# Products of zeros ahead of transposes and in waits of TensorE, in the third stretch of a two-layer decoder kernel

## The chip, the cores and the metric

The kernel runs on one core of a Trainium2 chip. The metric is the device time of one execution in microseconds (us), the median of some runs. TensorE does the matrix products and transposes, VectorE (DVE), ScalarE (ACT) and GpSimd (POOL) do the rest, SyncE (SP) issues most of the transfers. The profile also shows the clock that was granted to TensorE, as a share of 2.4 GHz; in each record it is either 1.0 or 0.5, that is 2.4 or 1.2 GHz.

## The reference

The input is 16 sequences of 128 tokens with 256 channels. Two layers follow each other, and each adds three blocks to the running x:

```python
x = x + L0_attn(layernorm(x))              # a gated convolution block
x = x + L0_xattn(ctx, layernorm(x), ctx)   # attention, queries from ctx
x = x + L0_ffn(layernorm(x))               # 32 experts, the best 2 of each token
x = x + L1_attn(layernorm(x))              # 16 causal heads
x = x + L1_xattn(layernorm(x), ctx, ctx)   # one wide head with an added bias
x = x + L1_ffn(layernorm(x))               # attention with rotary, then 8 experts
```

The change lies in the second layer. Its first block is causal attention in which the softmax is taken twice: once to find the entropy of each row, then again with the scores multiplied by a temperature that is a polynomial of that entropy.

```python
sim = einsum('bhid,bhjd->bhij', q, k) / sqrt(hd); sim = where(causal, neg, sim)
p = softmax(sim); entropy = -sum(p * log(p + 1e-9))
beta = where(entropy > 0.5, maximum(poly(entropy), 1.0), 1.0)
out = einsum('bhij,bhjd->bhid', softmax(sim * beta), v) @ Wo.T + bo
```

Its third block begins with a causal attention without temperature, with rotary position factors, and ends with 8 experts of which each token takes 2.

## The kernel before

The program has three stretches. The first does the first two blocks of layer 0, the second the 32 experts. The third (`phase_c`, line 1578) does all of layer 1 and starts about 671 us after the first instruction; near its end the tiles of the 8 experts follow (`Tiles`, line 2314), which end the program.

The third stretch works on eight pairs g = 0 to 7, two sequences each. A pair passes through six parts, and each part has a program of its own for each engine: `first` (norm, transposes, the products q, k and v), the attention `one` with temperature, `mix` (output product, the wide-head attention), `rotary` (norm, q, k and v of the third block), the attention `two`, and `last` (output product, gate of the experts). The transposes of `first`, `mix`, `rotary` and `last` are those of line 253; the products with the weights have lines 272 and 281.

An attention works through four units u = 0 to 3 of a pair (`UNITS`, line 286): one sequence and half of the heads each, so eight heads. For one unit TensorE does, in `causal_tensor` (line 1444):

- `sc`: the mask by two bf16 products (line 1466) and the scores by two f32 products (line 1468) into two banks of its result memory;
- `tr`: eight transposes of the exponentials (line 1486) into the same two banks;
- `pv`: eight products with the values (line 1498), into the bank `bs`;
- `ot`: two transposes back (line 1504).

Between them VectorE takes the maximum (line 1523), divides an earlier output (lines 1537 and 1539) and subtracts the maximum (line 1529); ScalarE takes the exponential (line 1556), copies the transposed exponentials out of the banks (line 1559) and copies the output (line 1563). In attention `one` there is more between the subtraction and the last exponential: ScalarE's exponential and logarithm (lines 1762 and 1767), VectorE's sums (lines 1779 and 1784), and on GpSimd two wide products (lines 1796 and 1799), ten small operations of the polynomial (lines 1802 to 1817) and the wide product with the temperature (line 1820).

All units of attention `one` share one pair of banks. So the scores of unit u of the next pair can be written only when the transposes of unit u of this pair have been copied out, and the transposes of unit u + 1 only when VectorE has subtracted the maximum from those scores (lines 1478 to 1484). In the first two pairs this gives a fixed turn: transposes of unit u of pair 0, copy, values, scores of unit u of pair 1, maximum, subtraction, transposes of unit u + 1 of pair 0.

Each engine's order is fixed: `emit` and `weave` (lines 104 to 115) merge the programs of all parts by the times of the table `AT_C` (line 1297), and the engines then run in that order; the table's times are used for nothing else. An f32 product stands in the trace as two records, a transpose as one.

`keep_warm(c, con, n, bank)` (line 1082) issues n products of a tile of zeros with itself, 128x128 by 128x256 in f32, into a bank whose content is not read after it. The kernel before has 37 of them: at the start of the program, around the border of the second and third stretch, and in the first pairs.

Of the kernel before, what the change touches and what calls it, by code (L numbers as in the profile page):

```python
# [24 lines left out]
NG = NSEQ // GS  # L25
# [34 lines left out]
class Tally:  # L60
# [9 lines left out]
    def at(self, n, j=None):  # L70
        return self.sem, self.base + self.step * (self.per * n + (self.per if j is None else j + 1))
# [32 lines left out]
def weave(plans):  # L104

    plans = [[next(p, None), p] for p in plans]
    while plans := [x for x in plans if x[0] is not None]:
        first = min(plans, key=lambda x: x[0])
        yield first[0]
        first[0] = next(first[1], None)  # L110
# [971 lines left out]
def keep_warm(c, con, n, bank=7):  # L1082

    for _ in range(n):
        c.nc.tensor.matmul(c.ps[:, bank, 0:D], con["zero"][:, 0:P], con["zero"][:, 0:D], start=True, stop=True, skip_group_check=True)
# [355 lines left out]
    return tally.at(n, j)  # L1441


def causal_tensor(c, l, con, g, at, woven):


    pe, ps = c.nc.tensor, c.ps

    def scores(u):
        s, ch = UNITS[u]  # L1450
        b0 = l.place(g, u).b0
        yield at("sc", u)
        if u == 0:
            pe.wait_ge(*l.q_in.at(g))
            pe.wait_ge(*l.k_in.at(g))
        if woven:
            if u:
                pe.wait_ge(*l.dd.at(g, u - 1))
            if g:
                pe.wait_ge(*l.pt_in.at(g - 1, u))  # L1460
        elif u == 1 and l.apart(g):
            pe.wait_ge(*l.other.pt_in.at(g))
        elif u or g:
            pe.wait_ge(*earlier(l.pt_in, g, u, 2 if u and l.apart(g) else 1))
        for b in range(2):
            pe.matmul(ps[:, b0 + b, :], con["ident_bf"], con["mask"], start=True, stop=True, skip_group_check=True)
        for b in range(2):
            m = pe.matmul(ps[:, b0 + b, :], l.qt[64 * b:64 * b + 64, ch, P * s:P * s + P], l.kp[64 * b:64 * b + 64, ch, :, P * s:P * s + P],  # L1468
                          start=False, stop=True, tile_position=(64 * b, 0), skip_group_check=True)
        m.then_inc(*l.sc.up())  # L1470
        if woven and g == 0 and u == 1:
            keep_warm(c, con, 2, 5)

    def values(u):
        s, ch = UNITS[u]
        d, there = l.d[u % l.n_d], l.place(g, u)
        yield at("tr", u)
        pe.wait_ge(*l.ee.at(g, u))
        if woven and u == 0:
            pe.wait_ge(*l.dd.at(g))  # L1480
        elif woven:
            pe.wait_ge(*l.pt_in.at(g, u - 1))
            if g + 1 < NG:
                pe.wait_ge(*l.dd.at(g + 1, u - 1))
        for h in range(NU):
            m = pe.transpose(ps[:, there.b0 + h // 4, P * (h % 4):P * (h % 4) + P], d[:, h, :], con["ident"])  # L1486
        m.then_inc(*l.tr.up())
        yield at("pv", u)
        pe.wait_ge(*l.pt_in.at(g, u))
        if u == 0:  # L1490
            pe.wait_ge(*l.v_in.at(g))
        if u == 1 and l.apart(g):
            pe.wait_ge(*l.other.ao_in.at(g))
        elif g or u:
            pe.wait_ge(*earlier(l.ao_in, g, u, 2 if u and l.apart(g) else 1))
        for h in range(NU):
            r, half = h % 4, h // 4
            m = pe.matmul(ps[32 * r:32 * r + 32, there.bs, P * half:P * half + P], l.vv[:, s, NU * ch + h, :], d[:, h, :],  # L1498
                          start=True, stop=True, tile_position=(0, 32 * r), skip_group_check=True)
        m.then_inc(*l.pv.up())  # L1500
        yield at("ot", u)
        pe.wait_ge(*l.os_in.at(g, u))
        for half in range(2):
            m = pe.transpose(ps[:, there.bs, P * half:P * half + P], there.os[:, P * half:P * half + P], con["ident"])
        m.then_inc(*l.ot.up())

    def in_order(part):
        for u in range(len(UNITS)):
            yield from part(u)

    yield from weave([in_order(scores)] + [values(u) for u in range(len(UNITS))])


# [64 lines left out]
def phase_c(c, con, dram, persist, w, arena, results, tables, tiles, xd_zero):  # L1578
# [7 lines left out]
    tick = lambda g: (lambda piece, u="": AT_C["%s%s" % (piece, u)][g])  # L1586
    tick_b = lambda g: (lambda piece, u: AT_C["%s%db" % (piece, u)][g])
    TOP, MIX = 7, 6
    with ExitStack() as ctx:
# [85 lines left out]
        def first_tensor(g):  # L1675
            at = tick(g)
            yield at("t0")
            if g == 0:
                pe.wait_ge(*comb.at(g))
                keep_warm(c, con, 3)  # L1680
                pe.wait_ge(*first.mean.at(g))
                keep_warm(c, con, 2)
            pe.wait_ge(*first.xn.at(g))
            if g:
                pe.wait_ge(*one.v_in.at(g - 1))
            if g >= 4:
                pe.wait_ge(*lg_in.at(g - 4))
                if g % 2:
                    pe.wait_ge(*router.pr_in.at(g // 2 - 2))
            turn_rows(c, first, con, x_first)  # L1690
            yield at("q")
            pe.wait_ge(*first.xt_in.at(g))
            by_channel(c, TOP, w.wa[:, 0, :, :], first.xt).then_inc(*qpj.up())
            yield at("k")
            pe.wait_ge(*one.q_in.at(g))
            by_channel(c, TOP, w.wa[:, 1, :, :], first.xt).then_inc(*kpj.up())
            yield at("v")
            pe.wait_ge(*one.k_in.at(g))
            by_token(c, TOP, w.wa[:, 2, :, :], first.xt).then_inc(*vpj.up())

# [254 lines left out]
        def rotary_tensor(g):  # L1955
            at = tick(g)
            yield at("t3")
            pe.wait_ge(*rot.xn.at(g))
            turn_rows(c, rot, con, x_rms)
            yield at("rk")  # L1960
            pe.wait_ge(*rot.xt_in.at(g))
            for k in range(KD):
                m = pe.matmul(ps[:, MIX, 0:GT], w.wk[:, k, :], rot.xt[:, k, :], start=(k == 0), stop=(k == KD - 1), skip_group_check=True)
            m.then_inc(*rk.up())
            yield at("rr")
            pe.wait_ge(*kr_in.at(g))
            for ch in range(KD):
                m = pe.matmul(ps[:, MIX, GT * ch:GT * ch + GT], w.rep[0:4 * HD, ch, :], kr[0:4 * HD, :], start=True, stop=True, skip_group_check=True)  # L1968
            m.then_inc(*rr.up())
            for half in range(2):  # L1970
                yield at("rq%d" % half)
                if half == 0:
                    pe.wait_ge(*two.k_in.at(g))
                else:
                    pe.wait_ge(*rq_half.at(g))
                by_channel(c, MIX, w.wf[:, half, :, :], rot.xt).then_inc(*rq.up())
            yield at("rv")
            pe.wait_ge(*two.q_in.at(g))
            by_token(c, MIX, w.wv, rot.xt).then_inc(*rv.up())
# [66 lines left out]
        def last_tensor(g):  # L2046
            at = tick(g)
            yield at("t5")
            pe.wait_ge(*two.ao_in.at(g))
            pe.wait_ge(*one.v_in.at(min(g + 3, NG - 1)))  # L2050
            if g:
                pe.wait_ge(*lg_in.at(g - 1))
                if g == NG - 2:
                    pe.wait_ge(*tables.cnt_in.at(0))
                if g % 2 == 0 or g == NG - 1:
                    pe.wait_ge(*router.pr_in.at((g + 1) // 2 - 1))
            turn_rows(c, last, con, two.ao)
            yield at("o2")
            pe.wait_ge(*last.xt_in.at(2 * g))
            by_token(c, TOP, w.wf[:, 2, :, :], last.xt).then_inc(*oj2.up())  # L2060
            yield at("t6")
            pe.wait_ge(*rows_in.at(g))
            turn_rows(c, last, con, rows[g % 2][:, :, 0:D])
            yield at("gate")
            pe.wait_ge(*last.xt_in.at(2 * g + 1))
            by_token(c, TOP, w.gw, last.xt).then_inc(*lg_mm.up())
# [92 lines left out]
                        in_=rows[s // GS][:, s % GS, :], in_offset=None).then_inc(*s_disp[s // GS].up())  # L2159

        def tensor_program(g):
            yield from weave([first_tensor(g), causal_tensor(c, one, con, g, tick(g), True), mix_tensor(g), rotary_tensor(g),
                              causal_tensor(c, two, con, g, tick_b(g), False), last_tensor(g)])

        def vector_program(g):
            yield from weave([first_vector(g), causal_vector(c, one, g, tick(g), mix.turned.at(2 * g - 2) if g else None, temperature_vector(g)),
# [36 lines left out]
        def tables_tensor():  # L2203
            for n, choice in enumerate((NROUND - 2, len(CHOICES) - 1)):
                yield settled[n] + LATE * n
                pe.wait_ge(*router.pr_in.at(choice))
                pe.wait_ge(*meta.at(choice))
                tables.count_tensor(c, con, total, TOP)
# [511 lines left out]
```

## Time and profile before

| | us |
|---|---|
| median of 3 runs | 1454.74 (1453.48 to 1459.05) |
| the profiled execution, time | 1466.06 |
| the profiled execution, span from first to last instruction | 1463.2 |
| TensorE busy in the span | 1312.7 (90%) |
| VectorE, ScalarE, GpSimd busy | 779.7, 689.0, 536.1 |
| mean granted clock of TensorE | 0.963 |

The page of the profile cuts the span into 40 slices of 36.6 us and gives for each the busy share of the engines and the granted clock in tenths; "9" is 90% or more. A window view gives the same for stretches of one's own choice. A timeline gives the instructions of one engine in order, and in brackets how long the engine sat idle before one, and what ended that wait.

### The profile page before, as it was taken

The page shows a single profiled execution, that of the slowest core. Times are in us where ns is not written, and L with a number is a line of the kernel's source. Part 1 is how long each engine was busy: PE and PEld are TensorE (multiplying, and loading weights), DVE is VectorE, ACT ScalarE, POOL GpSimd, SP SyncE. Part 2 cuts the span into 40 slices and gives each one's busy share as a digit, 9 for nine tenths or more (in the row PEclk, how much of TensorE's full clock was granted, in tenths as well). Part 3 has the DMA queues.
Part 4 walks back from the last instruction along what each step waited for, and adds up shares of the span by engine and source line. Part 5 has one row for each costly group of instructions (what it writes and reads, how often), then busy time and mean ns, then how long its engine had stood idle before and what let it go on. Part 6 is the DMA issues. An engine that isn't in the chain of part 4 may idle for free. (4 is left out here: it accounts for less than half of the span.)

```text
span 1463.2 us, 23121 instructions
## 1 busy us (share of the span) xinstructions
PE 1312.7 (90%) x8464; PEld 989.9 (68%) x8464; DVE 779.7 (53%) x1791; ACT 689.0 (47%) x1254; POOL 536.1 (37%) x777
## 2 busy tenths in 40 slices
PE   9899999988999999896667989989989779999996
PEld 7576767757999999894334665656656545666664
DVE  4876868673111111113656687977776645433332
ACT  6454747552222222222447687768777445222221
POOL 2123130402000000006878887887867033322222
PEclk9999999999999999998869999999999989999998
DMA  9673563903877777713000001000010634322221
GB/s 352 252 200 106 123 166 106 230 12 124 292 264 264 262 267 280 279 48 98 19 1 5 20 29 33 20 29 20 0 48 16 243 97 136 60 39 41 44 39 11
DMA packets 70686, 171.00 MB, mean 117 GB/s; under 512 B 8508, under 2 KB 47425, under 8 KB 60464
## 3 DMA queue, kind: packets, MB, share of 16 engines
q1 hardware_dynamic: 54944, 144.39, 30.9%
q0 software_dynamic: 10224, 16.09, 5.3%
q10 hardware_dynamic: 5408, 9.04, 1.7%
q8 instruction: 69, 1.13, 0.3%
q14 instruction: 41, 0.34, 0.1%
HBM read 123.11 MB, written 48.07 MB: 117 GB/s over the span
## 5 line engine op out<-in xcount | busy, mean ns | idle before, releaser
L1187 ACT ACTIVATE b_ht<-ps,b_b 128x154 f32<-128x154 f32 x256 | 85.4, 387 | 205.8 <-PE ps L1154 189.5
L1202 DVE TENSOR_SCALAR b_yt<-ps,b_b 128x154 f32<-128x154 f32 x64 | 21.2, 373 | 244.0 <-PE ps L1167 244.0
L2309 POOL DMA_INDIRECT experts<-ye,gidx_all x32 | 32.1, 1002 | 325.2 <-SPq L1093 314.6
L2384 PE MATMUL ps<-experts,d_xt 128*128 x312 | 147.1, 594 | 1.2 <-ACT d_xt L2440 0.8
L1154 PE MATMUL ps<-b_xet,ring 128*128 128x154 f32 x1024 | 143.7, 298 | 3.7 <-ACT b_ht L1187 3.7
L1154 PEld LDWEIGHTS ps<-b_xet,ring 128*128 128x128 f32 x1024 | 138.3, 192 | 3.9 <-issue 3.8
L1167 PE MATMUL ps<-b_ht,ring 128*128 128x154 f32 x1024 | 139.7, 294 | 0.4 <-DVE b_yt L1202 0.4
L1167 PEld LDWEIGHTS ps<-b_ht,ring 128*128 128x128 f32 x1024 | 136.3, 189 | 0.6 <-issue 0.6
L2526 POOL DMA_INDIRECT out_dram<-d_yd,d_to x39 | 60.6, 1554 | 158.5 <-DVE d_yd L2498 151.2
L1523 DVE TENSOR_REDUCE c_mx<-ps 128x8 f32<-128x1024 f32 x64 | 77.8, 1215 | 63.8 <-PE ps L1468 63.3
L1486 PE MATMUL ps<-cf,experts 128*128 128x128 f32 x512 | 73.3, 290 | 24.8 <-DVE experts L1529 12.6
L1486 PEld LDWEIGHTS ps<-cf,experts 128*128 128x128 f32 x512 | 61.5, 149 | 37.0 <-ACT experts L1556 18.4
L2384 PEld LDWEIGHTS ps<-experts,d_xt 128*128 128x128 f32 x312 | 56.0, 190 | 41.0 <-issue 39.0
L1799 POOL TENSOR_TENSOR experts<-experts 128x1024 f32<-128x1024 f32 x32 | 75.4, 2360 | 13.3 <-ACT experts L1767 13.3
L1559 ACT ACTIVATE experts<-ps 128x1024 f32<-128x1024 f32 x64 | 65.4, 1023 | 30.7 <-PE ps L1486 26.0
L235 POOL TENSOR_SCALAR a_rs<-a_mv 128x2 f32<-128x2 f32 x24 | 6.0, 250 | 200.3 <-DVE a_mv L190 200.3
L1529 DVE TENSOR_TENSOR experts<-ps,c_mx 128x1024 f32<-128x1024 f32 x64 | 78.1, 1220 | 1.6 <-PE ps L1498 0.2
L1468 PE MATMUL ps<-experts 64*128 64x512 f32 x256 | 78.7, 694 | 0.0
L1556 ACT ACTIVATE experts<-experts 128x1024 f32<-128x1024 f32 x64 | 67.5, 1057 | 22.9 <-DVE experts L1529 13.3
L2402 PE MATMUL ps<-experts,d_gt 128*128 x312 | 73.9, 380 | 0.9 <-DVE d_gt L2479 0.9
L2447 ACT ACTIVATE d_gs<-ps 128x512 f32<-128x512 f32 x39 | 23.3, 597 | 105.4 <-PE ps L2384 102.4
L1796 POOL TENSOR_TENSOR experts<-experts,c_zz 128x1024 f32<-128x1024 f32 x32 | 60.7, 1898 | 14.3 <-DVE c_zz L1781 14.0
(336 smaller groups left out, 2839.0 us busy)
## 6 DMA issues: line engine op xcount, KB each, us to landing
ring<-in_w SPq DMA_DIRECT2D x64, 1024.0 KB, 5.4
xd<-zero SPq DMA_DIRECT2D x6, 3120.0 KB, 25.9
a_kp<-in_ctx_k SPq DMA_DIRECT2D x8, 1024.0 KB
experts<-in_wd SPq DMA_DIRECT2D x1, 7424.0 KB
d_xd<-xd SPq DMA_DIRECT2D x39, 130.0 KB, 2.1
xe<-zero SPq DMA_DIRECT2D x1, 4928.0 KB, 33.2
b_xe<-xe SPq DMA_DIRECT2D x32, 154.0 KB
ye<-b_ye ACTq DMA_DIRECT2D x32, 154.0 KB
```

The lines of the kernel that those rows point to most:

```text
L1154: r = pe.matmul(ps[:, b, CAP * (m % 2):CAP * (m % 2) + CAP], w1r[:, slot, k, P * m:P * m + P], xet[:, e % 2, k, :], start=(k == 0), stop=( ...
L1167: r = pe.matmul(ps[:, 5, CAP * j:CAP * j + CAP], w2r[:, slot, m, P * j:P * j + P], ht[:, e % 2, m, :], start=(m == 0), stop=(m == MF0 - 1) ...
L1187: r = a.activation(ht[:, e % 2, m, :], ps[:, b, CAP * (m % 2):CAP * (m % 2) + CAP], ACT.Gelu, bias=b1[:, e, m:m + 1])
L1468: m = pe.matmul(ps[:, b0 + b, :], l.qt[64 * b:64 * b + 64, ch, P * s:P * s + P], l.kp[64 * b:64 * b + 64, ch, :, P * s:P * s + P], start=F ...
L1486: m = pe.transpose(ps[:, there.b0 + h // 4, P * (h % 4):P * (h % 4) + P], d[:, h, :], con["ident"])
L1523: v.tensor_reduce(l.mx[u][:, :], both, AX, ALU.max).then_inc(*c.dv.up())
L1529: v.tensor_tensor(l.d[u % l.n_d][:, :, :], both, l.mx[u][:, :, None].to_broadcast([P, NU, P]), ALU.subtract).then_inc(*l.dd.up())
L1556: a.activation(d[:, :, :], d[:, :, :], ACT.Exp).then_inc(*l.ee.up())
L1559: a.activation(d[:, :, :], l.scores(c, g, u), ACT.Copy).then_inc(*l.pt_in.up())
L1799: pool.tensor_tensor(e, e, l, ALU.mult).then_inc(*pr.up())
L2384: m = pe.matmul(ps[:, b, :], xt[:, j % 2, k, :], w13[:, bass.ds(e, 1), f:f + F1], start=(k == 0), stop=(k == KD - 1))
L2402: m = pe.matmul(ps[:, 4, 0:D], gt[:, j % 2, f, :], w2[:, bass.ds(e, 1), D * f:D * f + D], start=(f == 0), stop=(f == MF1 - 1))
```

## The change

Ten calls of `keep_warm` are added, 51 products of zeros in all. Each call stands ahead of the wait of the instruction group that follows it. In attention `one` a table says how many go ahead of the transposes of which pair and unit: 4, 5, 5, 5 for the four units of pair 0 and 4 for unit 0 of pair 1, all into bank 5. In `first` of pair 1, 4 go ahead of the product k and 5 ahead of the product v. In the last pairs, 9 go ahead of the transposes of unit 2 of attention `two` of pair 6, 6 ahead of the first rotary q product of pair 7, and 4 ahead of the count for the expert tables, all into bank 0.

```diff
-def causal_tensor(c, l, con, g, at, woven):
+def causal_tensor(c, l, con, g, at, woven, warm):
...
         yield at("tr", u)
+        keep_warm(c, con, *warm.get((g, u), (0, 0)))
         pe.wait_ge(*l.ee.at(g, u))
...
             yield at("k")
+            if g == 1:
+                keep_warm(c, con, 4, 5)
             pe.wait_ge(*one.q_in.at(g))
             by_channel(c, TOP, w.wa[:, 1, :, :], first.xt).then_inc(*kpj.up())
             yield at("v")
+            if g == 1:
+                keep_warm(c, con, 5, 5)
             pe.wait_ge(*one.k_in.at(g))
...
                 yield at("rq%d" % half)
                 if half == 0:
+                    if g == NG - 1:
+                        keep_warm(c, con, 6, 0)
                     pe.wait_ge(*two.k_in.at(g))
...
-            yield from weave([first_tensor(g), causal_tensor(c, one, con, g, tick(g), True), mix_tensor(g), rotary_tensor(g),
-                              causal_tensor(c, two, con, g, tick_b(g), False), last_tensor(g)])
+            yield from weave([first_tensor(g), causal_tensor(c, one, con, g, tick(g), True, {(0, 0): (4, 5), (0, 1): (5, 5), (0, 2): (5, 5), (0, 3): (5, 5), (1, 0): (4, 5)}), mix_tensor(g), rotary_tensor(g),
+                              causal_tensor(c, two, con, g, tick_b(g), False, {(NG - 2, 2): (9, 0)}), last_tensor(g)])
...
                 yield settled[n] + LATE * n
+                if n == 0:
+                    keep_warm(c, con, 4, 0)
                 pe.wait_ge(*router.pr_in.at(choice))
                 pe.wait_ge(*meta.at(choice))
                 tables.count_tensor(c, con, total, TOP)
```

## Rows read from the trace of the kernel before

**Rows 1.** The page, part 2: the clock granted to TensorE, by slices.
```profile
PEclk9999999999999999998869999999999989999998
```

**Rows 2.** Windows: us, busy by engine (instructions), granted clock, DMA share, GB/s.
```profile
724.32:734.40 10.08, 6.35 (x32) 3.02 (x33) 4.58 (x8) 3.72 (x5) 9.41 (x18) 0.66 0.00 1
734.40:744.26 9.86, 6.24 (x32) 2.85 (x33) 5.16 (x7) 3.41 (x5) 8.73 (x20) 0.65 0.00 0
744.26:760.51 16.25, 11.96 (x63) 5.28 (x63) 7.73 (x9) 8.22 (x10) 10.81 (x15) 0.52 0.00 1
```

**Rows 3.** Timeline of TensorE, pairs 0 and 1: start, us, line, tiles, [idle before].
```profile
719.62 2.47 PE L281 MATMUL ps<-weights,c_xt_f 128*128 128x256 f32 x8 [2.51 <-ACT experts L1574]
724.32 1.97 PE L1486 MATMUL ps<-cf,experts 128*128 128x128 f32 x8 [2.22 <-ACT experts L1556]
727.40 1.08 PE L1498 MATMUL ps<-experts 128*32 128x128 f32 x16 [1.11 <-ACT experts L1559]
728.41 1.03 PE L1466 MATMUL ps<-cb 128*128 128x512 bf16 x2
729.37 2.04 PE L1468 MATMUL ps<-experts 64*128 64x512 f32 x4
731.34 0.44 PE L1504 MATMUL ps<-cf,c_os 128*128 128x128 f32 x2
734.40 1.71 PE L1486 MATMUL ps<-cf,experts 128*128 128x128 f32 x8 [2.62 <-DVE experts L1529]
...
753.47 1.94 PE L1486 MATMUL ps<-cf,experts 128*128 128x128 f32 x8 [2.06 <-DVE experts L1529]
...
760.51 1.11 PE L253 MATMUL ps<-cf,experts 128*128 128x128 f32 x4
```

**Rows 4.** The same timeline somewhat later, at full clock.
```profile
768.55 1.04 PE L1486 MATMUL ps<-cf,experts 128*128 128x128 f32 x8
770.72 1.99 PE L281 MATMUL ps<-weights,c_xt_f 128*128 128x256 f32 x8 [1.13 <-ACT experts L1574]
772.64 0.64 PE L1498 MATMUL ps<-experts 128*32 128x128 f32 x16
773.22 0.61 PE L1466 MATMUL ps<-cb 128*128 128x512 bf16 x2
773.76 1.13 PE L1468 MATMUL ps<-experts 64*128 64x512 f32 x4
```

**Rows 5.** The same timeline: products of zeros, two records each.
```profile
660.13 2.32 PE L1085 MATMUL ps<-zero 128*128 128x256 f32 x10
...
698.43 2.07 PE L1085 MATMUL ps<-zero 128*128 128x256 f32 x4
```

**Rows 6.** Timeline of VectorE: maximum and subtraction of one unit.
```profile
731.46 1.23 DVE L1523 TENSOR_REDUCE c_mx<-ps 128x8 f32<-128x1024 f32 x1 [5.12 <-PE ps L1468]
...
733.04 1.21 DVE L1529 TENSOR_TENSOR experts<-ps,c_mx 128x1024 f32<-128x1024 f32 x1
```

**Rows 7.** Timeline of ScalarE: the exponential of unit 1 of pair 0.
```profile
731.40 1.06 ACT L1556 ACTIVATE experts<-experts 128x1024 f32<-128x1024 f32 x1 [0.70 <-POOL experts L1820]
```

**Rows 8.** Window of GpSimd: us, busy (instructions), clock, DMA share, GB/s.
```profile
742.69:772.61 29.92, 20.01 (x29) 0.71 0.01 1
```

**Rows 9.** Timeline of TensorE in the last pairs.
```profile
1164.58 0.17 PE L2237 MATMUL ps<-total,cb 128*128 128x8 bf16 x1 [2.30 <-DVE c_rows L2136]
...
1174.00 1.97 PE L1486 MATMUL ps<-cf,experts 128*128 128x128 f32 x8 [5.55 <-ACT experts L1556]
...
1188.25 3.78 PE L272 MATMUL ps<-c_xt_r,weights 128*128 128x256 f32 x8 [3.37 <-ACT experts L1574]
...
1192.81 1.99 PE L272 MATMUL ps<-c_xt_r,weights 128*128 128x256 f32 x8
```

**Rows 10.** Window of VectorE in the last pairs: columns as in Rows 8.
```profile
1164.78:1172.86 8.08, 7.43 (x25) 0.71 0.49 170
```

**Rows 11.** Timeline of ScalarE in the last pairs.
```profile
1175.02 0.91 ACT L2024 ACTIVATE c_x_rms<-c_x_rot,c_r_r 128x256 f32<-128x256 f32 x2
```

## The prediction

> **What bounds the kernel now.** I read the page's clock line first. The granted clock is at 90% or more nearly everywhere; it is lower in slices 19 to 21, where the third stretch begins, and a little in slice 33, where its last pairs run [rows 1]. There the change puts its work, so the next view is the windows of the turns of the first pairs: from 724.32 to 760.51 four units of pair 0 are turned, each with the scores of pair 1, and the clock was 0.66, 0.65 and, over the last two, 0.52 [rows 2]. A turn took 10.08, 9.86 and then 8.1 us.
>
> The timeline of TensorE shows what a turn is made of [rows 3]: eight transposes (1.97), a wait of 1.11 for ScalarE's copy, the products with the values (1.08), two mask products (1.03), the scores (2.04), two transposes back (0.44), and then a wait of 2.62 that VectorE's subtraction ends. In that wait VectorE takes the maximum (1.23) and subtracts it (1.21), with the division of an earlier output between them [rows 6]. Nothing in the turn lies beside anything else: TensorE waits for ScalarE, then VectorE waits 5.12 us for TensorE [rows 6], then TensorE waits for VectorE. So the length of TensorE's instructions is on the path here, though the engine is idle more than a third of the time. GpSimd is nearly as close: it is busy 9.41 of 10.08 us in the first turn and 8.73 of 9.86 in the second [rows 2].
>
> The same instructions at 2.4 GHz took 1.04, 0.64, 0.61 and 1.13 us [rows 4]: 3.42 together, against 6.12 at 1.2 GHz [rows 3]. At full clock a turn is 2.70 us shorter.
>
> **The zeros and their cover.** Ten records, five products of zeros, took 2.32 us at full clock, 0.46 each [rows 5]. Two took 2.07 at half clock, which includes the run-out of the last; I take twice the full-clock price, 0.93 each, as the lower end there and 1.03 as the upper. The added groups against the waits that they fall into, at full clock:
>
> - product v of pair 1: 5 cost 2.3, the wait is 2.51 [rows 3]; ahead of k there is a wait like it, and 4 cost 1.9. Both hidden.
> - transposes of unit 0: 4 cost 1.9 in 2.22. Of units 1, 2 and 3: 5 cost 2.3 in waits of 2.62, one between, and 2.06 [rows 3]. That wait is VectorE's work behind the scores and does not depend on TensorE's clock: 1.23 + 1.21 and about half a us of division, less the 0.44 of transposes back. Hidden, with 0.3 to spare; in a wait of 2.06 they overrun by as much.
> - transposes of unit 0 of pair 1: TensorE comes to them without a wait, at 768.55, and 4 cost 1.9. Behind them it waits 1.13 for ScalarE [rows 4], which takes up that much; 0.7 stays. The ends are 0 and 1.9; I take 0.7 lost.
>
> At half clock every group of five is 4.7 us and overruns its wait by about 2. That is the case in which the change costs time (below).
>
> **What the first pairs give.** The transposes of unit 0 stay where they are, at 724.32, since their exponential releases them [rows 3]. Unit 1 would come 2.70 earlier by TensorE, but its exponential starts at 731.40, when GpSimd has given the temperature, and takes 1.06 [rows 7]. So its transposes start at 732.5 instead of 734.40: 1.9 gained. Units 2 and 3 and what follows at 760.51 can gain 2.70 each: 10.0 in all. Work of GpSimd bounds this as well: from 742.69 to 772.61 it is busy 20.01 of 29.92 us, so its own chain can't move forward by more than 9.9 [rows 8]. The lower bound of this part is nothing gained.
>
> I don't take the whole. Where unit 1 has to wait for its exponential, TensorE is idle behind the zeros, does 1 us of transposes and is idle again for the copy. In the turns of before the clock, once up, fell again in just such idle stretches: the means of 0.66 and 0.65 are mixtures of 1.0 and 0.5 [rows 2]. One pass of values, masks and scores at half clock costs 4.15 instead of 2.38, so 1.77. I count two such passes of the four: 10.0 - 3.5 = 6.5. With the 0.7 lost in pair 1, the first pairs give 5.8 us. Behind them everything follows through waits on semaphores, with no fixed time, so what is gained by 770 should reach the end.
>
> The row of the transposes bears on this: eight of them took 1.04 us at full clock, half of the 1.97 at half clock [rows 3, 4], so they do run at 2.4 GHz. The Trainium skill, "TensorE: Matmul & The Clock Gate", section "Part 4: PE-mode transpose", says that the full clock doesn't engage for transposes, which do not count as busy. The first half of that this trace contradicts. The second half, if true, speaks against the change as placed right ahead of transposes, and is the rival "fallen again" below.
>
> **What the last pairs give.** Four zeros cost 1.9 ahead of the count, in a wait of 2.30; nine cost 4.2 in a wait of 5.55; six cost 2.8 in a wait of 3.37 [rows 9]. All hidden at full clock. At half clock they take 3.7, 8.4 and 5.6 and overrun by 1.4, 2.8 and 2.2. What gets shorter:
>
> - between the count and the nine zeros nothing: VectorE has 7.43 us of work in the 8.08 before the exponential, so it sets the date of the transposes at 1174.00 [rows 10, 9], whatever TensorE's clock.
> - these transposes go from 1.97 to 1.04, but what is next, the transposes of the rotary part at about 1176, waits for ScalarE's scaled rows, written from 1175.02 to 1175.93 [rows 11]. Nothing gained there; the masks and scores behind them can give up to 0.6.
> - the rotary q product took 3.78 at half clock; the same one four us later took 1.99 [rows 9]: 1.8 gained if the six zeros have the clock up by then. If they themselves run at half clock first, they end 2.2 late, and 0.4 is lost.
>
> The sum is between -0.4 and +2.4. I take half of the upper end, 1.2: TensorE is nearly idle before both groups, so part of the zeros will run at half clock.
>
> **Sum.** 5.8 + 1.2 = 7.0 us. Of the profiled execution, 1463.2 + 2.9 = 1466.06, that gives 1459.1. It is 11.3 above the median of the runs; carried over as a difference, the forecast is 1454.74 - 7.0 = 1447.7.
>
> **The rivals.**
>
> *The clock holds everywhere.* All four turns run at 2.4 GHz and the last pairs give all: 10.0 - 0.7 + 2.4 = 11.7, so 1443.0. For it: with zeros in it, a turn has TensorE busy 2.3 + 3.4 + 0.3 of some 7.4 us, and later, with the same instructions, the clock is up [rows 4]. Against it: GpSimd is within a quarter of a us of being the bound (9.9 against 10.0).
>
> *Fallen again.* The zeros lift the clock, transposes don't hold it, and it falls while ScalarE copies; values, masks and scores run at half clock in all four turns. 10.0 - 4 x 1.77 = 2.9, less 0.7, plus 1.2: 3.4 gained, 1451.3. For it: a gap of over 1 us stands on either side of the transposes of unit 1. Against it: in rows 4 a wait of 1.13 behind transposes left the clock up.
>
> *Absorbed.* The turns get shorter, but the temperature's work on GpSimd (busy 20.01 of 29.92 us right behind, and more in the first turns) sets the pace and the time is given back before pair 2. Only the last pairs gain: 1.2, so 1453.5. It decides if GpSimd has no wait left between 742 and 772; it had 9.9 us of them [rows 8], most behind work that itself waits for TensorE, which speaks against it.
>
> *Slower: the zeros hold TensorE.* The groups start at half clock and end after the wait that they should fill. By the rows above, if all ran at half clock, the overruns are 1.2 + 2.1 (k, v), 1.5 (unit 0), 2.0 three times, 2.6 (pair 1), 1.4, 2.8 and 2.2: 19.8 us. It decides where more than half of the groups run at 1.2 GHz; at half of them the price is 9.9, less half of the gain of 7.0: 6.4 slower, 1461.1. For it: in rows 5 zeros did run at half clock. Against it: a group that overruns has filled the wait, so the clock should be up for the next one.
>
> **How the numbers follow.** Chances: forecast 0.43, with a range of its own of 1445 to 1450; the clock holds 0.22; fallen again 0.16; absorbed 0.10; slower 0.09. Runs of this kernel differ by some 0.4%, so 0.5%, or 7.3 us, is what a measurement can tell from no change. The line is 1447.5, in the middle of the forecast's own range: half of it, 0.21, and the case above it, 0.22, make faster 0.43; the other half, 0.16 and 0.10 make within 0.5% 0.48 (rounded); slower 0.09. The range of 8 in 10 goes from 1442.5 to 1454: it leaves out the slower case and the far ends of the others.
>
> **What would show it.** Right: in the profile after, the 32 products of zeros in pairs 0 and 1 take 0.46 each; the transposes of units 1, 2 and 3 begin 8.2, then 7.2 to 9 us after one another and take about 1.0; the clock from 724 to 752 is over 0.8; transposes of unit 1 are released by ScalarE's exponential, not by VectorE; pair 2's first transposes stand at about 754. The waits ahead of the transposes are a few tenths. The rotary q product of pair 7 takes 2.0. Wrong: transposes at 1.0 with scores at 2.0 in each turn (fallen again); pair 2 no earlier than 759 with GpSimd busy throughout (absorbed); groups of zeros of over 4 us with no wait behind them (slower). A cold stretch that appears elsewhere in pairs 2 to 6, where the shift moves waits about, would change the sum by 1 to 3 us without any step being wrong.

## The result, and the profile after

| | before | after |
|---|---|---|
| median of 20 runs, us | 1460.95 (1453.48 to 1464.85) | 1450.73 (1443.23 to 1455.86) |
| ratio to before, with its 95% interval | | 0.9937 [0.9924, 0.9949] |
| profiled execution: span, clock | 1463.2, 0.963 | 1449.0, 0.975 |

By the ratio the kernel became 9.2 us faster (7.5 to 11.1); the forecast's 7.0 us of 1454.74 are a ratio of 0.9952. The forecast lies just outside that interval. The 20 runs of before have a higher median than the 3 that were shown, so the ratio is what to compare.

The clock line of the page after, to be held against [rows 1]: slices 20, 21 and 33 are at 9 again. Slice 19, which ends ahead of the turns, is still at 8. Slices 10 and 22 are at 8 now: in slice 22, behind the turns, the clock was at half for 10.2 us from 780.3 on.

```profile
PEclk9999999998999999998998999999999999999999
```

The windows of the turns after, with the columns of [rows 2]. The clock is 1.00 in all of them.

```profile
723.55:731.73 8.18, 5.71 (x42) 3.64 (x43) 4.43 (x7) 3.67 (x5) 7.64 (x14) 1.00 0.01 3
731.73:739.16 7.43, 5.86 (x42) 3.66 (x43) 5.31 (x7) 3.47 (x5) 6.43 (x20) 1.00 0.00 0
739.16:750.61 11.45, 8.91 (x72) 5.26 (x73) 5.79 (x8) 8.03 (x9) 11.20 (x10) 1.00 0.00 0
```

The timeline of TensorE after answers to [rows 3]. The first turn went from 10.08 to 8.18 us, the second from 9.86 to 7.43, the last two together from 16.25 to 11.45. The transposes of unit 1 are now released by ScalarE's exponential (line 1557 here, 1556 before), and those of unit 3 have no wait left.

```profile
723.55 1.09 PE L1487 MATMUL ps<-cf,experts 128*128 128x128 f32 x8 [0.41 <-ACT experts L1557]
...
728.20 2.32 PE L1085 MATMUL ps<-zero 128*128 128x256 f32 x10
731.73 1.09 PE L1487 MATMUL ps<-cf,experts 128*128 128x128 f32 x8 [1.20 <-ACT experts L1557]
...
739.16 1.06 PE L1487 MATMUL ps<-cf,experts 128*128 128x128 f32 x8 [0.46 <-DVE experts L1530]
...
746.26 1.06 PE L1487 MATMUL ps<-cf,experts 128*128 128x128 f32 x8
...
750.61 0.66 PE L253 MATMUL ps<-cf,experts 128*128 128x128 f32 x4
...
758.19 1.89 PE L1085 MATMUL ps<-zero 128*128 128x256 f32 x8
```

The last pairs after, to be held against [rows 9]: the rotary q product takes 1.89 instead of 3.78, while the transposes behind the nine zeros still take 1.97.

```profile
1154.21 0.17 PE L2246 MATMUL ps<-total,cb 128*128 128x8 bf16 x1 [0.39 <-DVE c_rows L2143]
...
1156.34 4.05 PE L1085 MATMUL ps<-zero 128*128 128x256 f32 x18
1163.64 1.97 PE L1487 MATMUL ps<-cf,experts 128*128 128x128 f32 x8 [3.25 <-ACT experts L1557]
...
1173.32 2.86 PE L1085 MATMUL ps<-zero 128*128 128x256 f32 x12
1176.01 1.89 PE L272 MATMUL ps<-c_xt_r,weights 128*128 128x256 f32 x8
```

Between the same instructions of the two traces the stretches are:

| stretch | before, us | after, us | gained |
|---|---|---|---|
| start to the transposes of unit 0, pair 0 | 724.32 | 723.55 | 0.8 |
| to the first transposes of pair 2 (four turns) | 36.19 | 27.06 | 9.1 |
| to the count (pairs 2 to 6) | 404.07 | 403.60 | 0.5 |
| to the second rotary q product of pair 7 | 28.23 | 24.47 | 3.8 |
| to the end | 270.34 | 270.32 | 0.0 |

These are 14.2 us for one execution of each, 5 more than the ratio of all runs gives. The profiled execution of before took 1466.06, 5.1 above the median of its 20 runs, while the one after took 1450.80, which is its median. Part of the 3.8 is not the zeros' doing. In the trace of before, ScalarE copied an output of attention `two` 2.0 us after the values were ready (TensorE ended them at 1180.96), at the end of a wait that is put down to a transfer; in the trace after, the wait there is 3.74 and ends with TensorE. This is ScalarE's timeline before:

```profile
1182.94 0.39 ACT L1563 ACTIVATE c_os<-ps 128x256 f32<-128x256 f32 x1 [4.97 <-DMA a_vv<-in_ctx_v]
```

### The profile page after: what moved, and what is told of

Its sections match the earlier page's. It is cut to its first block and busy times, and to the rows that moved or that the text cites. A ratio compares the mean times of both kernels' runs of the same rounds, so it can differ in the third digit from the quotient of the medians.

```text
span 1449.0 us, 23284 instructions
## 1 busy us (share of the span) xinstructions
PE 1318.6 (91%) x8525; PEld 1005.0 (69%) x8566; DVE 780.6 (54%) x1791; ACT 688.5 (48%) x1254; POOL 535.3 (37%) x777
## 3 DMA queue, kind: packets, MB, share of 16 engines
q1 hardware_dynamic: 54944, 144.39, 31.1%
## 5 line engine op out<-in xcount | busy, mean ns | idle before, releaser
L1468 PE MATMUL ps<-experts 64*128 64x512 f32 x256 | 75.0, 663 | 0.0
```

## The experiments

Each was timed in 5 rounds beside the kernel before on the same chip; three chips were used, so ratios are compared and not times. "Turns" is the stretch of the second row of the table above, "last pairs" that of the fourth; both are of one profiled execution. The kernel before has 36.2 and 28.2, the changed one 27.1 and 24.5.

| kernel | zeros kept or changed | ratio, 95% | turns | last pairs |
|---|---|---|---|---|
| first_only | pairs 0 and 1 alone | 0.9969 [0.9945, 0.9992] | 27.1 | 25.9 |
| last_only | last pairs alone | 0.9986 [0.9965, 1.0007] | 34.4 | 24.2 |
| no_pair1 | without the 4 of pair 1, unit 0 | 0.9929 [0.9909, 0.9949] | 27.1 | 24.5 |
| turned | transposes of zeros instead | 0.9938 [0.9915, 0.9962] | 28.5 | 24.5 |
| double | 10 for 5 in units 1 to 3 | 0.9947 [0.9928, 0.9965] | 31.1 | 24.2 |
| fewer | 2 for 5 in units 1 to 3 | 0.9943 [0.9930, 0.9957] | 29.4 | 24.3 |
| plus12 | no_pair1, and 6 for pair 1, unit 2 | 0.9920 [0.9907, 0.9932] | 27.1 | 24.4 |
| no_nine | without the 9 of the last pairs | 0.9909 [0.9893, 0.9926] | 28.7 | 24.3 |
| again | the changed kernel | 0.9928 [0.9905, 0.9951] | 28.7 | 25.5 |
| best | plus12 and no_nine in one | 0.9900 [0.9877, 0.9923] | 28.6 | 27.3 |
| no_kv0 | without those of k, v, unit 0 | 0.9934 [0.9909, 0.9960] | 29.0 | 25.5 |
| six_only | the 6 of the last pairs alone | 0.9987 [0.9965, 1.0008] | 34.2 | 27.3 |

**Which half carries the gain.** `first_only` and `last_only` keep one half of the edit each.

```diff
 # first_only
-causal_tensor(c, two, ..., {(NG - 2, 2): (9, 0)})
+causal_tensor(c, two, ..., {})
-                    if g == NG - 1:
-                        keep_warm(c, con, 6, 0)
-                if n == 0:
-                    keep_warm(c, con, 4, 0)
 # last_only
-causal_tensor(c, one, ..., {(0, 0): (4, 5), ..., (1, 0): (4, 5)})
+causal_tensor(c, one, ..., {})
-            if g == 1:
-                keep_warm(c, con, 4, 5)     # and the 5 of v
```

> Only the 32 products of zeros in pairs 0 and 1 stay; the 19 of the last pairs are gone. Theory (the turns of the first pairs carry the gain): from the transposes of unit 0 of pair 0 to pair 2's first transposes 27 us as in the changed kernel (36.2 before), and a ratio to the kernel before of 0.9945 to 0.9955 (6.5 to 8 us). Rival (the last pairs carry half of it): ratio 0.997.

> Only the 4, 9 and 6 products of zeros of the last pairs stay. Theory: the first turns are as long as before (36 us for four), the rotary q product of pair 7 takes 1.9 instead of 3.8, and the kernel is 1 to 2 us faster than before, ratio 0.9986 to 0.9993. Rival (the 3.8 us that the last pairs gained in the changed kernel's trace are the zeros' doing): ratio 0.9974.

The turns follow the zeros of pairs 0 and 1: 27.1 with them, 34.4 without in `last_only`. In `six_only`, which has none there either, they take 34.2. So of the three traces without these zeros that of before has the longest turns. `first_only` measured 4.5 us faster than before (1.2 to 8.0), less than expected, and the other half 2.0 (-1.0 to 5.1). The intervals overlap, so the ratios rank the halves only weakly; the traces place them. Without zeros the last pairs take 25.9 in `first_only`, and 26.2 in the trace of before if the 2.0 of ScalarE's late copy are taken off. With zeros and without the late copy they take 24.2 to 24.5 in eight traces, and 25.5 in `again` and `no_kv0`, where the half clock behind the nine zeros reached the product that follows the scores (1.93 and 2.07 us instead of 1.13). So against `first_only` they give 1.5 to 1.7 us in most executions and 0.4 in some; 2.0 of the 3.8 was the late copy.

**The four zeros of pair 1.** `no_pair1` takes `(1, 0): (4, 5)` out of the table.

> As the changed kernel, without the 4 products of zeros ahead of the transposes of unit 0 of pair 1. Theory: they cost 1.3 us in the changed kernel's trace (the shift fell from 9.90 to 8.63) and 1.1 of that came back by the next unit, so the kernel takes the same as the changed one within 0.5 us, ratio 0.9935. Rival (they hold the clock up for what follows): slower by 1 to 3 us, ratio 0.995 or more. Second rival (a plain cost): 1.3 us faster than the changed kernel, ratio 0.9928.

In the changed kernel these transposes come 9.31 us behind pair 2's first ones, without the four 7.58. By unit 1 it is 18.21 and 18.20. The 1.7 us that they add are given back whole within one unit, where before TensorE waited 1.13 for ScalarE [rows 4]: in the trace they cost nothing and do nothing. The ratio, 0.9929 [0.9909, 0.9949], speaks against the first rival's 0.995; it can't tell the theory from the plain cost of 1.3 us.

**Do transposes hold the clock?** `turned` issues transposes of the zero tile, four for each product of zeros, in the same places.

```diff
+def keep_turned(c, con, n, bank):
+    for _ in range(4 * n):
+        c.nc.tensor.transpose(c.ps[:, bank, 0:P], con["zero"][:, 0:P], con["ident"])
...
-        keep_warm(c, con, *warm.get((g, u), (0, 0)))
+        keep_turned(c, con, *warm.get((g, u), (0, 0)))
```

The expectation excepts the nine of the last pairs; in the kernel that ran they were replaced too, so all ten groups are transposes.

> Each added product of zeros in the ten places (but the nine of the last pairs, which stay as they are counted in the same way ahead of transposes) is replaced by four transposes of the zero tile, which take about as long: 20 for a group of five, 2.3 us at full clock. Theory (transposes don't count as work for the clock): the transposes of units 1 to 3 take 1.7 to 2.0 again and the four turns 34 us or more; the groups of twenty take over 4 us at half clock and the kernel is as slow as before or slower, ratio 0.998 to 1.006. Rival (any busy TensorE holds the clock): turns of 27 us, ratio 0.9937.

The theory fell. These are the windows of its first three turns (columns of [rows 2]):

```profile
724.46:732.65 8.19, 5.88 (x52) 4.03 (x53) 4.44 (x7) 3.67 (x5) 7.65 (x14) 1.00 0.01 3
732.65:741.52 8.87, 7.32 (x52) 4.49 (x53) 5.31 (x7) 3.47 (x5) 7.62 (x23) 0.81 0.00 0
741.52:748.62 7.10, 5.86 (x53) 4.04 (x53) 3.99 (x5) 5.38 (x6) 7.10 (x4) 1.00 0.01 2
```

The first and third are as fast as with products; in the second the clock fell to 1.2 GHz for 3.4 us at 734.6, in the wait for ScalarE's copy that follows the wait for the exponential. The same fall stands in the second turn of `again`, `no_nine` and `best`, whose groups are products. In the fourth turn it stayed at 2.4 GHz. The measured ratio is that of the changed kernel.

**How much to fill.** `double` writes 10 for 5 in the table's units 1 to 3, `fewer` writes 2.

> As the changed kernel, with 10 products of zeros instead of 5 ahead of the transposes of units 1, 2 and 3 of pair 0, so 4.6 us in waits of 2.6. Theory (a wait is free only as long as it is; what is over it holds TensorE): each of the three turns gets 2.0 to 2.3 us longer, 9.5 to 9.8 instead of 7.4, and pair 2's first transposes come 5 to 6 us later than in the changed kernel; ratio 0.997 to 0.998. Rival (only the clock counts, GpSimd sets the pace of the turns): turns as in the changed kernel, ratio 0.9937.

> As the changed kernel, with 2 products of zeros instead of 5 ahead of the transposes of units 1, 2 and 3 of pair 0, 0.9 us each. Theory (the wait has to be filled nearly whole, since TensorE idles 1.1 us behind the transposes too): the clock falls in at least two of the three turns, transposes or scores at twice their time, turns of 8.5 to 10 us, pair 2's first transposes 3 to 6 us later than in the changed kernel, ratio 0.996 to 0.998. Rival (the zeros ahead of k, v and unit 0 raised the clock, and little is needed to hold it): turns of 7.4 us, ratio 0.9937.

Windows of the first three turns of `double`, then of `fewer`:

```profile
723.24:732.22 8.98, 7.86 (x53) 5.68 (x54) 4.44 (x7) 4.46 (x5) 8.44 (x14) 1.00 0.01 3
732.22:741.13 8.91, 7.80 (x53) 5.62 (x52) 5.87 (x8) 3.62 (x5) 7.65 (x23) 1.00 0.00 0
741.13:750.05 8.92, 7.80 (x54) 5.62 (x53) 4.84 (x7) 4.32 (x5) 8.70 (x5) 1.00 0.01 2
```

```profile
726.57:734.77 8.20, 4.57 (x36) 2.50 (x37) 4.44 (x7) 3.66 (x5) 7.65 (x14) 0.96 0.00 0
734.77:744.51 9.74, 6.87 (x36) 3.68 (x37) 5.31 (x7) 3.47 (x5) 8.49 (x23) 0.68 0.01 3
744.51:751.61 7.10, 4.55 (x37) 2.51 (x37) 3.99 (x6) 5.37 (x6) 6.89 (x5) 1.00 0.00 0
```

With ten, every turn is 8.9 to 9.0: the zeros take 4.48 us, the second and third turns are 1.5 and 1.8 us longer than the changed kernel's, and the turns together 4.1 us. The mechanism is as expected, its price a little less, and in the first turn only 0.8, since there ScalarE's exponential sets the date anyway. With two, one turn of three fell to half clock, not two; the sum is 2.3 us longer. But with five the clock fell once as well in `again`, `no_nine` and `best`, at 1.6 us, so one trace of `fewer` doesn't show that two hold the clock less well. How full the wait has to be stays open. In both the ratio shows less of this than the trace, within its interval.

**The first thirteen.** `no_kv0` drops `keep_warm` ahead of k and v and the entry `(0, 0)`.

> As the changed kernel, without the products of zeros ahead of k, v and the transposes of unit 0 of pair 0 (13 of the 51). Theory (these only bring the clock up before the turns): the first turn starts at half clock and is 9 to 10 us long, the first five zeros take over 4 us, the second and third are as in the changed kernel (7.4); the loss is 2 to 3 us, ratio 0.9955. Rival (the zeros of units 1 to 3 do it all): ratio 0.9937, four turns in 27 us.

The first turn is 10.11 us, at half clock, the second and third 7.41 and 7.09. Its five zeros took 2.32, at full clock, not over 4: the clock rose at 732.2, behind the values, masks and most of the scores, and the zeros began at 732.56. The loss in the turns is 1.9 us against 27.1, close to the 2 to 3 expected, though hardly more than the difference between two executions of the changed kernel (27.1 and 28.7). What speaks for the thirteen is that the first turn ran at half clock only here, of all kernels with zeros in these pairs. The ratio, 0.9934, is that of the rival; with its interval it can't tell 2 us.

**The nine, and the six.** `no_nine` empties the table of attention `two`; `six_only` keeps nothing but the six.

> As the changed kernel, without the 9 products of zeros ahead of the transposes of unit 2 of attention two of pair 6. Theory (VectorE sets the date of these transposes, and what follows them waits for ScalarE): from the count to the second rotary q product of pair 7 24.5 to 25 us as in the changed kernel (24.47), ratio 0.9937. Rival (they hold the clock for what follows): 1 to 2 us slower there, ratio 0.995.

> Only the 6 products of zeros ahead of the rotary q product of pair 7 stay. Theory: from the count to the second rotary q product 24.5 us against 25.9 with none, so the six alone are the gain of the last pairs: 1 to 1.5 us faster than before, ratio 0.999 to 0.9993. Rival (without the four ahead of the count the six start at half clock, overrun the wait by 2 us and gain nothing): 26 us or more, ratio 1.000.

Without the nine the last pairs take 24.3, as long as with them. The ratio, 0.9909, is lower than expected, but what this trace gains lies in pairs 2 to 6, ahead of the nine (below), so they can't be its cause. Whether leaving them out makes the kernel faster isn't shown. TensorE's timeline of `no_nine` has the transposes at half clock, as in the changed kernel, and the rotary q product at full clock:

```profile
1160.19 1.97 PE L1487 MATMUL ps<-cf,experts 128*128 128x128 f32 x8 [7.13 <-ACT experts L1557]
...
1172.35 1.89 PE L272 MATMUL ps<-c_xt_r,weights 128*128 128x256 f32 x8
```

In `six_only` the six products began at half clock and took 4.54 us, 1.7 more than in the changed kernel, and the rotary q product behind them 1.89. The late copy of ScalarE (a wait of 4.97, as before) is in this trace too and adds 2 us, so 27.3 is 25.3 without it, and 28.2 before is 26.2: about 0.9 gained. The overrun takes half of what the product gains. That the four ahead of the count are missing isn't shown to be the reason: `best` has them, and its six took 4.54 us too. What the two traces share is the late copy: shortly ahead of the six TensorE stood idle for it 2.50 us in `six_only` and 2.36 in `best`, and 0.51 in the changed kernel.

**A better placement.** `plus12` and `best` put six ahead of unit 2 of pair 1, where TensorE waits 3.02 us in the changed kernel, with the clock at half from 780.3 on for 10.2 us.

```diff
-{(0, 0): (4, 5), ..., (0, 3): (5, 5), (1, 0): (4, 5)}
+{(0, 0): (4, 5), ..., (0, 3): (5, 5), (1, 2): (6, 5)}
```

> As the changed kernel, without the 4 products of zeros of unit 0 of pair 1 and with 6 (2.8 us) ahead of the transposes of unit 2 of pair 1, where TensorE waits 3.02 us and the clock falls behind it in every trace so far (3.4 to 10.2 us at half). Theory: no half clock between 775 and 795, transposes of unit 3 of pair 1 come 2 us earlier than in the changed kernel (788.83 there), ratio 0.991 to 0.9925. Rival (GpSimd sets the pace there, its wide products are back to back): same within 0.5 us, ratio 0.9930 as without the four.

> The changed kernel itself, for comparison with the others of this chip. Theory: ratio 0.9937, as measured, within 0.0015; turns of 27.1 us from the transposes of unit 0 of pair 0 to pair 2's first transposes.

> As the changed kernel, without the 4 products of zeros of unit 0 of pair 1 and the 9 of the last pairs, with 6 ahead of unit 2 of pair 1. Theory (the four cost up to 1.3 us, the nine give nothing, the six keep the clock through unit 2 of pair 1): 2 to 4 us faster than the changed kernel, ratio 0.990 to 0.992. Rival (what the runs without four and without nine gained was where the clock happened to fall in pairs 2 to 6): ratio 0.9925 to 0.994.

TensorE's timeline of `plus12`: the six fit, and no half clock is left between 709.5 and 1037.2 us.

```profile
776.32 2.76 PE L1085 MATMUL ps<-zero 128*128 128x256 f32 x12
779.50 1.06 PE L1487 MATMUL ps<-cf,experts 128*128 128x128 f32 x8 [0.43 <-DVE experts L1530]
...
787.15 1.04 PE L1487 MATMUL ps<-cf,experts 128*128 128x128 f32 x8
```

From unit 2 to unit 3 it is 7.65 us there, 10.08 in the changed kernel's first trace and 8.5 in `again`, where the clock was at half for 3.4 us. `again` has the expected ratio, though its turns took 28.7 and not 27.1. `best` has the lowest ratio of all, 0.9900, and on its chip a median of 1453.13 beside 1456.53 of `again`; the intervals overlap, so that it beats the changed kernel is possible and not shown. Its trace happens to have ScalarE's late copy.

**What moves the rest.** The stretch from pair 2 to the count holds few of the edits: the four of pair 1 or the six of `plus12`, and the four ahead of the count. Yet it takes 397.2 us in `no_nine`, 403.6 in the changed kernel, 404.1 before and 407.9 in `no_kv0`. Two things go with this. The first is the clock. In nine of the fourteen traces the stretch goes with the time that it spends at half clock: 397.2 and 397.6 us with 10 us of it, 399.7 to 400.6 with 14 to 23, 403.4 to 403.7 with 27.

The second is a wait that the clock doesn't explain. In before, `again`, `best`, `no_kv0` and `six_only` ScalarE and VectorE start 1.2 to 3.3 us late at 944 to 956 us, and the profile shows no releaser ("remote"). TensorE had ended the transposes that ScalarE copies here at 941.94. These are ScalarE's and VectorE's timelines of `again`:

```profile
946.26 1.02 ACT L1560 ACTIVATE experts<-ps 128x1024 f32<-128x1024 f32 x1 [3.33 <-remote]
946.30 0.21 DVE L1538 RECIPROCAL c_rz<-ps 128x8 f32<-128x8 f32 x1 [2.37 <-remote]
```

With this wait the stretch takes 401.8 us in `again`, at 10 us of half clock, and 407.9 in `no_kv0`, at 27, so some 4 us more than in traces without it. The four kernels with it besides before all ran on the third chip, and of the nine traces without it none did; what it is wasn't found.

Over the 20 runs of the changed kernel, span and mean clock have a correlation of -0.92: the two runs at 0.973 have spans of 1453.6 and 1454.1 us, the one at 0.983 has 1441.4. So executions of one program differ by 10 us and more, and most of that goes with the granted clock. It is why ratios of 5 to 12 runs have intervals 4 to 7 us wide here, and why terms of 1 or 2 us had to be read in traces, of which there is one for each kernel.

## Why the prediction was right

This line of TensorE's timeline before, the transposes of unit 2, goes with the first point:

```profile
744.26 1.36 PE L1486 MATMUL ps<-cf,experts 128*128 128x128 f32 x8 [2.50 <-DVE experts L1529]
```

- *TensorE's length is on the path of a turn, 2.70 us of it at full clock, 10.0 in all.* Right in kind, 0.9 too high: the second, third and fourth turns lost 2.43, 2.11 and 2.69, so the whole was 9.1. The transposes of units 1 and 2 were partly at full clock already, at 1.71 [rows 3] and 1.36 us. And the trace that was shown had longer turns than the two others without zeros there (36.2 against 34.4 and 34.2), so on average there was less still to gain.
- *Unit 1 waits for its exponential, so its turn gives 1.9.* Right to a tenth: 10.08 became 8.18, released by ScalarE.
- *Two of four passes at half clock, 3.5 us off.* Mis-sized. In seven traces with the changed kernel's own groups in pair 0 (the changed kernel, `again`, `first_only`, `no_pair1`, `plus12`, `no_nine`, `best`) no pass was in four, which took 27.1, and one in three, which took 28.6 to 28.7. One pass costs 1.6, so the term should have been 0 to 1.6, some 0.7 on average. The means of the seven (27.7) and of the three without zeros (34.9) give 7.2 for the turns; single pairs of traces give 5.6 to 9.1.
- *The four zeros of pair 1 lose 0.7.* Nothing is lost.
- *The nine gain nothing, since VectorE sets the date.* Right: from the count to those transposes 9.42 us before and 9.43 after [rows 9], and the same without them.
- *The rotary q product gains up to 1.8, the last pairs 1.2.* Right: the product went from 3.78 to 1.89, and the last pairs gain 0.4 to 1.7. The mean of the ten traces with zeros and without the late copy is 24.6, so 1.4 against `first_only`.
- *Groups fit their waits at full clock.* Right: 2.32, 1.89, 4.05 and 2.86 us of products; what wait is left is 0 to 1.2 us in the first pairs and 3.25 us behind the nine.
- *What is gained reaches the end.* By the ratio, yes; in single traces pairs 2 to 6 add up to 4 or take up to 7 us against the trace of before. Pair 2's first transposes came at 750.61, and not at about 754.

The sum by these sizes is 7.2 plus 1.4, so 8.6 us against 9.2 measured (7.5 to 11.1). The forecast of 7.0 came as near as it did because two errors had opposite signs: the ceiling of 10.0 was 0.9 too high for the trace shown and 2.1 on average, and the 3.5 and 0.7 taken off it were some 3.5 too many. That is luck in part; the mechanism is what was right. The rival *the clock holds everywhere* was nearer in what happened in the turns, though its 11.7 is above what was measured. GpSimd did become nearly the bound, as it said: the 29 instructions of [rows 8], which took 29.92 us, took 20.98 after, and GpSimd was busy for 19.81 of them.

```profile
741.89:762.87 20.98, 19.81 (x29) 1.00 0.00 1
```

*Absorbed* did not happen: pair 2 came 9.9 us earlier. Of *slower*, no group in pairs 0 and 1 ran at half clock in the changed kernel's trace; the six began so in `six_only` and `best`, at 4.54 us. *Fallen again* has no support: values, masks and scores ran at half clock in no turn of the changed kernel's trace and in one of four in `again`. The Trainium skill, "TensorE: Matmul & The Clock Gate", section "Part 4: PE-mode transpose", says that the full clock doesn't engage for transposes and that they don't count as busy as products do. `turned` contradicts both: its groups of transposes ran at full clock (20 in 2.35 us), and with them the clock stayed up in three turns of four, as in `again` with products.

## What to carry to other kernels

Where TensorE's own length is on a chain that returns to it through other engines, products of zeros in its waits paid here, with groups a little shorter than the wait at full clock; twice the group cost 0.8 to 1.8 us each time. Whether a smaller group holds the clock as well isn't settled. Put them where TensorE's own length, and no other engine, sets the date of what follows: ahead of transposes that VectorE released late anyway, nine products changed nothing in the trace. When a kernel's executions differ by 10 us, judge such an edit by the stretch between two of its own instructions, and by the ratio of many runs only for the whole.

## What the runs showed of the hardware

Transposes of a zero tile kept TensorE's clock at 2.4 GHz about as f32 products did (turns of 28.5 us against 27.1 to 28.7, ratios 0.9938 and 0.9937; without either the turns took 34.2 to 36.2). Transposes of other data weren't tried in their place. The clock fell without a long wait: in the second turn of `again` it fell at 735.4, behind two waits of 1.23 and 1.11 us with 1.09 us of transposes between them.

In 3 of 14 traces (before, `six_only` and `best`) ScalarE's copy at 1171 to 1183 us came 2 us after TensorE had released it, and in 5 of 14 ScalarE and VectorE started 1.2 to 3.3 us late near 950 us; what held them wasn't found.
